# Attention beside a channel mix, in one kernel: an even count of maximum pieces in every step, earlier loads of q and k, another form of the shift chain, and no loop over the groups

## The reference

```python
xn = _layernorm(x)
q, k, v = split(xn @ w_in.T)                  # 16 heads of 16
att = (q @ k.T) / 4
att = jnp.where(causal, att, 0.0)             # masked scores are 0, not -inf
att = softmax(att)
attn = (att @ v) @ w_out.T
r = sigmoid((mu_r*xn + (1-mu_r)*xn_prev) @ W_r.T)
k2 = square(relu((mu_k*xn + (1-mu_k)*xn_prev) @ W_k.T))
x = x + attn + r * (k2 @ W_v.T)
```

## Time and profile before

| | us |
|---|---|
| median of 3 runs | 1241.39 |
| the three runs | 1232.92, 1241.39, 1243.44 |
| the profiled execution's own time | 1247.56 |
| its span in the profile | 1245.8 |
| first exponential of the attention stage | 243.76 |
| last exponential | 1228 |
| PE, DVE, ACT, POOL busy | 1140.9, 950.6, 743.8, 347.6 |
| mean granted clock of PE, as a share of full | 0.968 |

### The profile page before, as it was taken

One profiled execution on the slowest core, in us unless ns is written; L12 is line 12 of the kernel. 1 busy time (PEld: TensorE's weight loads), 2 busy tenths in 40 slices (PEclk: granted clock), 3 DMA queues, 4 the chain that ended last, 5 costly groups with the idle time before them and its releaser, 6 DMA issues.

```text
span 1245.8 us, 26838 instructions
## 1 busy us (share of the span) xinstructions
PE 1140.9 (92%) x7168; PEld 472.1 (38%) x7168; DVE 950.6 (76%) x2433; ACT 743.8 (60%) x1553; POOL 347.6 (28%) x716
## 2 busy tenths in 40 slices
PE   6899888799999999989899999998999999999998
PEld 3666444433333233323333333232333332333345
DVE  5677888687799689858787789677886887789723
ACT  3444433257766666666557766665677657665773
POOL 2221113333223312331233323321334233324221
PEclk9999999799999999989899999999999999999999
DMA  3668533237005500550037004600180037002033
GB/s 126 192 165 190 184 118 102 69 39 107 6 2 64 87 6 2 66 86 6 4 41 111 6 2 53 98 6 4 29 122 7 2 41 111 6 2 77 5 105 108
DMA packets 62397, 79.67 MB, mean 64 GB/s; under 512 B 7075, under 2 KB 52515, under 8 KB 61219
## 3 DMA queue, kind: packets, MB, share of 16 engines
q1 hardware_dynamic: 61091, 73.66, 29.9%
q0 software_dynamic: 1152, 4.19, 1.1%
...
## 4 chain that ended last, share of the span: by engine, by line
PE 54%; issue 13%; DVE 9%; POOL 2%; DVEq 1%; ACT 1%; POOLq 0%; DMA 0%; SPq 0%; ACTq 0%
PE ps_o L1101 17%; PE ps_s L1087 16%; PE ps_m L236 15%; DVE part_max L251 3%; PE ps_m L1133 2%; PE ps_o L1111 2%; DVE ps_m L247 2%; POOL after L228 1%; DVE row_max L264 1%; DVE part_max L247 1%; PE ps_x L1078 1%; PE ps_x L1079 1%; ACT probs L969 1%; DVE turned L1004 1%; PE ps_x L1064 1%
## 5 line engine op out<-in xcount | busy, mean ns | idle before, releaser
L969 ACT ACTIVATE probs<-ps_s 128x512 f32<-128x512 f32 (+3 forms) x1280 | 610.5, 535 | 315.5 <-PE ps_s L1087 310.7
L251 DVE TENSOR_REDUCE part_max<-ps_m 128x1 f32<-128x512 f32 x730 | 474.6, 681 | 36.8 <-PE ps_m L236 35.1
L1087 PE MATMUL ps_s<-q_op,k_op 99*128 99x512 bf16 (+3 forms) x1280 | 437.3, 360 | 16.8 <-issue 8.1
L236 PE MATMUL ps_m<-k_op,q_op 96*128 96x512 bf16 (+3 forms) x1200 | 407.5, 359 | 34.0 <-DVE part_max L251 24.4
L247 DVE CUSTOM_DVE_ANT_0 ps_m<-ps_m,mask 128x384 f32<-128x384 f32 x470 | 229.7, 497 | 143.6 <-PE ps_m L236 141.4
L1101 PE MATMUL ps_o<-probs,v_sb 128*32 128x512 f32 (+3 forms) x2560 | 307.2, 553 | 9.6 <-POOL probs L917 9.6
L917 POOL TENSOR_SCALAR_AFFINE_SELECT probs<-probs 128x128 f32<-128x128 f32 x512 | 143.2, 296 | 414.7 <-ACT probs L969 408.1
L1087 PEld LDWEIGHTS ps_s<-q_op,k_op 99*128 99x128 bf16 x1280 | 122.8, 98 | 340.1 <-ACT probs L969 219.6
L236 PEld LDWEIGHTS ps_m<-k_op,q_op 96*128 96x128 bf16 x1200 | 118.7, 99 | 191.7 <-DVE part_max L251 85.7
L884 POOL TENSOR_TENSOR diag_weight<-ident,masked_weight 128x2048 f32<-128x2048 f32 x32 | 115.5, 3609 | 123.3 <-ACT masked_weight L936 123.3
L1101 PEld LDWEIGHTS ps_o<-probs,v_sb 128*32 128x32 f32 x2560 | 51.2, 109 | 101.2 <-issue 41.5
...
## 6 DMA issues: line engine op xcount, KB each, us to landing
...
v_sb<-vpad_d SPq DMA_DIRECT2D x8, 1024.0 KB, 26.4
...
attn_t<-normed SPq DMA_DIRECT2D x128, 32.0 KB, 2.3
```

What stands on the lines that cost most here:

```text
L236: last = pe.matmul(ps_m[:, f % ring, 0:width], self.q_op[0:ROWS, p, h, q0:q0 + P], self.k_op[0:ROWS, p, h, pc * CH:pc * CH + width], start ...
L251: dve.tensor_reduce(self.part_max[:, u % 2, h * SUB + s, pc:pc + 1], ps_m[:, f % ring, 0:width], AX_X, ALU.max).then_inc(self.piece_reduce ...
L969: act.activation(probs[:, slot % PRING, 0:width], ps_s[:, slot % SRING, 0:width], ACT.Exp).then_inc(probs_ready, 1)
L1087: pe.matmul(ps_s[:, slot % SRING, 0:CH - q0], k_op[0:KROWS, p, h, kt * P:(kt + 1) * P], q_op[0:KROWS, p, h, u * CH + q0:(u + 1) * CH], sta ...
```

## The change

1. **Pieces.** `pieces_of` and its tables go. `piece_at(u, kt, h)` gives one piece for each score tile, four in each of the 40 steps. The next group's pieces begin in step (2,7) instead of (3,0): units 0 to 2 take the last 76 pieces of the group up to (2,6), the rest of unit 2 takes 20 pieces of the next group and unit 3 takes 64. The token stage makes 84 pieces of group 0 instead of 80.
2. **Chain.** All five steps behind the first reduction become `scalar_tensor_tensor`. Where there was one tensor (the scaling at L268, the cast at L275), the second is now `floor`, zeros in SBUF.
3. **Loads.** The loads of q and k for the next group (`load_scores`) go to the begin of the group in SP's program, behind a wait for the last score tile of the group before. The load of v stays where it was.
4. **Shift.** The next group's unit 0 is turned in (3,3) instead of (3,5), unit 1 in (3,10) instead of (3,11).
5. **Loop.** The attention stage's loops over i are Python loops on all five engines: all eight groups are written out. The token stage's loop stays.

```diff
-HEAD_START = PIECE0[2] + 32
-SLOT_PIECES = {0: (HEAD_START, PIECE0[3]), 1: (PIECE0[3], PIECE0[3] + 32),
-               2: (PIECE0[3] + 32, PIECES), 3: (0, HEAD_START)}
-SLOT_SPREAD = {0: 16, 1: 32, 2: 30, 3: 64}
+AHEAD_FROM = 19
+HEAD_START = PIECES - 4 * AHEAD_FROM
-SHIFT_AT = {(3, 5): 0, (3, 11): 1, (1, 2): 2, (2, 8): 3}
+SHIFT_AT = {(3, 3): 0, (3, 10): 1, (1, 2): 2, (2, 8): 3}
-def pieces_of(slot, head_step):
...
+def piece_at(u, kt, h):
+    ahead, f = divmod(HEAD_START + GH * (KT0[u] + kt) + h, PIECES)
+    return f, ahead
...
-            dve.tensor_tensor(self.row_max[:, u], self.raw_max[:], self.floor[:, :, u * SUB:(u + 1) * SUB],
-                              ALU.max).then_inc(self.max_ready, 1)
+            dve.scalar_tensor_tensor(self.row_max[:, u], self.raw_max[:], 1.0, self.floor[:, :, u * SUB:(u + 1) * SUB],
+                                     ALU.mult, ALU.max).then_inc(self.max_ready, 1)
...
-            dve.tensor_scalar(by_head[0], self.row_max[:, u], -1.0, None, ALU.mult).then_inc(self.hi_ready, 1)
+            dve.scalar_tensor_tensor(by_head[0], self.row_max[:, u], -1.0, self.floor[:, :, 0:SUB],
+                                     ALU.mult, ALU.add).then_inc(self.hi_ready, 1)
...
-            dve.tensor_copy(by_head[1], self.shift_rest[:]).then_inc(self.mid_ready, 1)
+            dve.scalar_tensor_tensor(by_head[1], self.shift_rest[:], 1.0, self.floor[:, :, 0:SUB],
+                                     ALU.mult, ALU.add).then_inc(self.mid_ready, 1)
...
             def group(i, p, first=False, last=False):
+                if not last:
+                    if not first:
+                        sp.wait_ge(scores_ready, (i * 2 + p) * SLOTS)
+                    ops.load_scores(sp, i + p, 1 - p)
                 if not first:
                     keep_normed(i - 1 + p, 1 - p, NCH - 1)
                 place_shift(p, 2, unit_of(i, p, 2))
                 if not last:
                     sp.wait_ge(out_ready, unit_of(i, p, 0) + 1)
-                    ops.load_group(sp, i + p, 1 - p)
+                    ops.load_values(sp, i + p, 1 - p)
...
-            with sp.Fori(0, B * CC - 1) as i:
+            for i in range(B * CC - 1):
                 group(i, 1)
                 group(i + 1, 0)
```

More of the change, by code:

```diff
@@ L78, in piece @@
     return u, h, s, pc, (CH if pc < u else P * (s + 1))
-def pieces_of(slot, head_step):
-    lo, hi = SLOT_PIECES[slot]
-    n, spread = hi - lo, SLOT_SPREAD[slot]
-    at = min(head_step, spread)
-    return range(lo + n * at // spread, lo + n * min(at + 1, spread) // spread)
+def piece_at(u, kt, h):
+    ahead, f = divmod(HEAD_START + GH * (KT0[u] + kt) + h, PIECES)
+    return f, ahead
 def pieces_beside_tokens(c, step):
@@ L193, in place_ones, with load_scores @@
         sp.dma_start(rows, self.one_row[:].unsqueeze(1).broadcast_to([KROWS - ROWS, 2 * GH * NT, P])).then_inc(self.ones_placed, 16)
-    def load_group(self, sp, i, p):
+    def load_scores(self, sp, i, p):
         for r in range(len(Q_PARTS)):
@@ L925, in _ @@
             group(0, 0, first=True)
-            with pool.Fori(0, B * CC - 1) as i:
+            for i in range(B * CC - 1):
                 group(i, 1)
@@ L988, in _ @@
             group(0, 0, first=True)
-            with act.Fori(0, B * CC - 1) as i:
+            for i in range(B * CC - 1):
                 group(i, 1)
@@ L1027, in group @@
                 for u in range(NCH):
-                    nxt = NCH if u == NCH - 1 else 0
-                    base = (G + (nxt > 0)) * PIECES
                     for hs in range(key_tiles(u) * GH):
-                        if not (nxt and last):
-                            for f in pieces_of(u, hs):
-                                ops.reduce_piece(dve, ps_m, MRING, f, base)
-                                ops.after_piece(dve, f, unit_of(i, p, nxt), base, f + 1 == PIECES)
+                        f, ahead = piece_at(u, hs // GH, hs % GH)
+                        if not (ahead and last):
+                            base = (G + ahead) * PIECES
+                            ops.reduce_piece(dve, ps_m, MRING, f, base)
+                            ops.after_piece(dve, f, unit_of(i, p, NCH * ahead), base, f + 1 == PIECES)
                         if NORM_AT <= hs < NORM_AT + NORM_STEPS and not (first and u == 0):
@@ L1047, in _ @@
             group(0, 0, first=True)
-            with dve.Fori(0, B * CC - 1) as i:
+            for i in range(B * CC - 1):
                 group(i, 1)
@@ L1143, in group @@
                     pe.wait_ge(shift_loaded[u % 2], (G * (NCH // 2) + u // 2 + 2) * SHIFTS)
-                    if nxt and not last:
-                        pe.wait_ge(q_loaded[1 - p], ops.loaded(1 - p, i + 1 + p))
-                        pe.wait_ge(k_loaded[1 - p], ops.loaded(1 - p, i + 1 + p))
                     for kt in range(key_tiles(u)):
@@ L1149, in group @@
                             score_tile(p, u, kt, h, G)
-                            if not (nxt and last):
-                                for f in pieces_of(u, kt * GH + h):
-                                    ops.score_piece(pe, ps_m, MRING, f, 1 - p if nxt else p, (G + (nxt > 0)) * PIECES)
+                            f, ahead = piece_at(u, kt, h)
+                            if not (ahead and last):
+                                if ahead and f == 0:
+                                    pe.wait_ge(q_loaded[1 - p], ops.loaded(1 - p, i + 1 + p))
+                                    pe.wait_ge(k_loaded[1 - p], ops.loaded(1 - p, i + 1 + p))
+                                ops.score_piece(pe, ps_m, MRING, f, 1 - p if ahead else p, (G + ahead) * PIECES)
                             if h == 2:
@@ L1181, in _ @@
             group(0, 0, first=True)
-            with pe.Fori(0, B * CC - 1) as i:
+            for i in range(B * CC - 1):
                 group(i, 1)
```

4 lines of the change are left out of this document (2 added, 2 removed).

## The result

The changed kernel takes **1266.39 us** (median of 6 runs, 1265.23 to 1269.9) against 1235.05 for the kernel before on the same chip (6 runs, 1232.92 to 1243.44): ratio 1.024, 95% interval [1.0205, 1.0275]. It is slower by 2.4%. The forecast was 1236 us, with a range of 1192 to 1258; the measured time lies above it. The profiled execution took 1265.23 us, so between the two profiled executions (1247.56 and 1265.23) lie 17.7 us, between the medians 31.3.

What follows compares the result with a forecast made beforehand. It saw PE busy 92% and DVE 76%, both nearly full in unit 3, with losses at the loop, v's lateness and POOL against DVE. Terms summed to -5.1 us, taken off the 1241.4 median: 1236 us, range 1192 to 1258.

Steps and rivals of the forecast that it cites:

- loop: Attention stage, written out: 6.5 us saved for each of two jumps back, -13.0 us; steps otherwise no faster.
- loads: Steps (2,10) to (3,0): early q and k let v land in unit 1, ending POOL's wait; -14.6 us over seven groups.
- pieces, unit 3: Unit 3 of groups 0 to 6: 64 pieces instead of 80, 4.3 us less a group; -30 us in all.
- pieces, end of unit 2: Last four steps of unit 2: sixteen added pieces, about +0.6, given back by (2,3); 0, bounds -1 and +2 a group.
- pieces, token stage: Token stage: four more pieces at 0.56 us, half beside other work; +1.5 us, bounds 0 to 2.2.
- chain, unit 1's begin, 8: Unit 2's chain in (0,3): third member held about 3.1 us by L884; +2.0 in each of eight groups, +16 us.
- chain, unit 3's begin, 7: Next unit 0's chain in (2,11): fourth or fifth member held 3 us, PE clock falls; +5 by seven groups, +35 us.
- Form: Chain's new instructions: no time in itself, still wait for POOL; the cast and scaling, reading one tensor, now read two.
- rival 2: The chain's new form doesn't wait for POOL, so both chain terms and today's price go: 1161 us; chance 0.07.
- Cost 0: SP's twelve early q and k issues, 6.5 us, fall where SP waits anyway and delay nothing: 0 us.
- 1: Rival: next unit 0's chain passes ahead of L884 harmlessly, so the +35 falls away: 1201 us; chance 0.15.
- Rival 3: Each of fifteen 3 us stops leaves PE at its lower clock for 6.9 us: +28, 1264 us; chance 0.15.

Runs made afterwards that it cites:

- the base of "The pieces alone": Kernel before with loop written out, early loads, new chain form and POOL's product in four parts; pieces and chains at their old places: 1204.24 us, ratio 0.9704.

## Why the prediction failed, point by point

The sum was made against the profiled execution of before, so the two profiled executions stand in the first column of what came (the windows by unit and step, added up over the groups). What v's waits cost before was taken from the base of "The pieces alone", in which v is early: 219.60 us for unit 2 of the seven groups and 42.74 for (3,0)+(3,1). Unit 2 of the seven groups before and after:

```profile
sum 236.49, PE 217.63 PEld 69.24 DVE 153.69 ACT 164.92 POOL 87.12; mean PE 31.09 PEld 9.89 DVE 21.96 ACT 23.56 POOL 12.45
sum 241.02, PE 226.38 PEld 75.56 DVE 203.14 ACT 166.09 POOL 89.98; mean PE 32.34 PEld 10.79 DVE 29.02 ACT 23.73 POOL 12.85
```

| Term | forecast | between the profiles | by timed runs |
|---|---|---|---|
| loop | -13.0 | -13.0 | -12.4; 13.3 put back |
| loads | -14.6 | -20.3 | -11 to -13, form included |
| pieces, unit 3 | -30 | -25.9 | |
| pieces, end of unit 2 | 0 | +21.4 | |
| pieces, token stage | +1.5 | +2.7 | all pieces, with the late chains: -4 |
| chain, unit 1's begin, 8 | +16 | +17.1 | |
| chain, unit 3's begin, 7 | +35 | +36.3 | both chains put late: -67 |
| sum | -5.1 | +18.3 (17.7 measured) | +31.3 measured |

- **The step that failed is "at the end of unit 2 ... 0".** It compared DVE's 9.0 us of new work with the 8.9 us that the steps took and called it hidden, with +2 a group as its bound. It came out at +3.1 a group (241.02 - 219.60 = 21.4 over seven). PE's 7.47 busy of 8.89 us stood in the earlier trace rows, and PE's work of the pieces, which the same paragraph takes off unit 3 at 0.2 a piece, was not added on the side where the pieces arrive. It also took those steps at the length that v's lateness gave them (8.89 in group 5, where 8.20 is left when v is early), so that part of the room it filled was the loads' gain, counted again.
- **The second is in the sum's last line.** The difference was worked out from one execution and taken off a median 6.2 us lower. That execution was 12.5 us above the median of before on the chip of this comparison, and 4 to 10 above those of the experiments. Its waits for v are part of the difference: 20.3 us go in it, 11 to 13 in timed runs. But only a part: in the two profiled executions without the loop the early loads and the form take 18.0 us off unit 2 and (3,0)+(3,1), and (1,0)+(1,1) take 5.9 more (71.7 to 77.6 over eight groups); why is open. The kernel after has no such waits and comes out at 1265.2 in its profile and 1266.4 as median. Against the profiled execution the sum was 1242.5; with +21 for unit 2 it would have been 1264.
- *Chain*: right in mechanism, place, member (third; fifth), length (3.4, 3.7 us) and price within 1.3 us a term. The parts were less exact than their sum: for unit 3 the +5 was 3 us of standing and 2 of clock, and PE stood for 2.77 us and ran 6.8 at half speed, which is 3.4, more together than the 5.2 that came out. All in all it is what makes the change slower: with the chains late the four-piece kernel runs in 1199.
- *Form*: right that it doesn't escape POOL, and rival 2 falls; that the one-input forms were safer was wrong.
- *Loop*: right. *Loads*: with v early and the pieces as before, the three steps (2,10) to (3,0) fell to 5.77 us and not to 6.44, which is 4.7 of the 5.7 us that this term gave beyond the forecast. "Cost 0" for the twelve issues held in the changed kernel; in the kernel before with its loop the same issues lost 7 us in all.
- *Pieces in unit 3*: 3.4 to 3.7 a group, for 4.3; near PE's price, as taken. The three steps that the prediction called DVE's had PE busy for 8.32 of 9.10 us too; twelve pieces instead of fifteen took 1.05 us off them, for 1.7.
- *Rivals*: 1 and 2 fell. Rival 3 gave about the right number, 1264, and is right on the clock behind the seven stops in unit 3 (6.8 us at half, for its 6.9), wrong behind the eight in unit 1 (3.3). But both terms of the chain came out at the forecast's prices, so its +28 is not what filled the gap; unit 2's pieces did most of that.

## What to carry to other kernels

Before you call moved work hidden, add it to every engine that does a part of it, at the place where it arrives: an idle engine beside a full one is no room. Short operations in SBUF that stand ahead of a piece on DVE belong where POOL isn't in a long operation; here a shift by twelve pieces was worth 67 us, five times what the loop cost. And take a difference worked out in one execution off that execution, above all when it removes a wait that varies.

## What the runs showed beside that

- Two stops of PE of 1.06 and 0.72 us, 0.5 us apart, were followed by some 10 us at its lower level (clock 0.53 and 0.54), more than the 6.8 us behind one stop of 2.77 us, and that of 3.31 us at unit 1's begin by 3.3 us only. With the next group's chain alone put late, PE's two stops at that place are the same as in the changed kernel (0.81 and 3.31 us), and were followed by 6.9 us at half speed (0.88 over 28.6 us in group 1) and 10.4 in group 2 (0.83 over 30.5). So a stop's length alone didn't set what it costs; only these stretches were seen, and no rule was tested.
- In one kernel DVE stood 12.61 and 7.70 us for its own issue behind a jump back, while the DMA engines were full. In the changed kernel with loops, with the same transfers beside the same jumps, it didn't, and a whole jump costs 6.6 us there; in the kernel before, without the transfers, it costs 6.2.
- A cast of 128x16 waits for POOL's product of 128x2048 as long (3.66 us) as an operation with two tensors (3.67 us).
